# Adding D*x with GpSimd from a spread row of D instead of with TensorE's diagonal product, in a fused MoE / selective-scan / MoE kernel

## The chip, the cores and the metric

The kernel runs on one core of a Trainium2 chip. The metric is the device time of one execution in microseconds (us); the median of several executions is given. The engines are called PE (TensorE), DVE (VectorE), ACT (ScalarE), POOL (GpSimd) and SP (SyncE, which issues most of the DMAs). Each of them works through its own list of instructions in order, and they meet only at semaphores.

## The reference, cut to what matters

x has 4 batches of 512 tokens with 256 channels. A mixture-of-experts layer, a selective scan and a second mixture-of-experts layer follow one another, each on normalised rows and each added to x:

```python
x = x + 0.5 * ffn(layernorm(x))
x = x + scan(layernorm(x))          # 16 states for each channel
x = x + 0.5 * ffn(layernorm(x))

def scan(x):                        # x is already normalised here
    ...
    h = dA_t * h + dBx_t            # for each time step
    y_t = sum_n h[:, :, n] * C_t[n]
    return y + x * D                # D: one number for each of 256 channels
```

The change concerns the last line alone, x * D.

## The kernel before, in words

Tokens lie in 16 tiles of 128 rows (`x_sb`, and the normalised rows in `xn_no`, called `xn` in the code); four tiles make a batch. The first layer ends at about 110 us of the profiled execution, the scan layer runs from there to about 330 us, and the second layer fills the rest.

The scan layer's main part treats 64 states, s = 16 b + n, for batch b = 0 to 3 and n = 0 to 15. All of it is laid out by hand in loops `scan(b)`, one for each engine, and the place of an `if` in such a loop is the place of the work in the engine's order. For one state:

- ACT makes the decay `da` (128 partitions x 1024, for the 256 channels as two halves `k` of 512 time steps) three states ahead, and most of the inputs `dbx_t`.
- PE turns or multiplies the inputs into PSUM, `turn_dbx(s + 2)`, two states ahead. This is L1033 (transposes) or, for 22 of the states, L1040 (a product with a diagonal).
- DVE runs the recurrence over time, L1426, `hs[s]` from `da` and PSUM. `hs` is a ring of four, so it may not be more than four states ahead of POOL.
- POOL multiplies by C, L526: `gs[s % 2] = hs[s] * c_sb`, with two buffers of `gs`. It waits for DVE's `hs[s]` (`sc_h`) and for PE's use of `gs[s - 2]` (`sc_tp`).
- PE turns `gs[s]` back to rows and accumulates it over the 16 states of a batch in the two PSUM banks `YA`: `add(s)`, L1057, which waits for POOL's `gs[s]` (`sc_g`). In PE's order it stands as ..., `turn_dbx(s + 2)`, `add(s - 1)`, `turn_dbx(s + 3)`, `add(s)`, ...

After the 16th `add` of a batch, DVE adds `YA` to the rows in `x_sb`: `add_y(b)`, L1462, which stands behind the second scan of the next batch (its n = 1). Beside this, DVE, ACT and PE prepare the next batch (projections, dt, normalisation). POOL's other work in the loop is one addition of rows (L515, in batch 0) and small steps of layer norm (L455, L456, L463, L464) behind n = 5 of batch 0 and n = 3 of the others.

x * D is made by PE in `skip(b, i)`, L1066, at n = 5 to 8 of each batch: for tile i, both halves k of the turned rows `xnT` are multiplied with D's diagonal `d_diag` (in `q_sb`) and accumulated into `YA` between the `add`s. POOL makes the diagonals once, L545, after the first layer. The data of an fp32 product pass PE twice here, so two `matmul` calls show up as four records.

Of the kernel before, what the change touches and what calls it, by code (L numbers as in the profile page):

```python
# [15 lines left out]
ALU = mybir.AluOpType  # L16
ACT = mybir.ActivationFunctionType
# [6 lines left out]
P = 128  # L24
# [3 lines left out]
def macaron_kernel(nc, x, w_xT, w_dtT, b_dt, a_log, d_skip, router_w, gate_w, up_w, down_w,  # L28
                   sh_gate_w, sh_up_w, sh_down_w, out):
    BATCH, L, D = x.shape  # L30
# [3 lines left out]
    KC = D // P  # L34
    LT = L // P
    GT = BATCH * LT
# [6 lines left out]
    NR = WHOLE + MIXED  # L43
# [23 lines left out]
    rows = [nc.dram_tensor(f"rows{r}", [TOK, WIDE[r]], F32, kind="Internal").ap() for r in range(RUNS)]  # L67
# [9 lines left out]
    with ExitStack() as ctx:  # L77
        def sb(name, shape, dt=F32):
            return ctx.enter_context(nc.sbuf_tensor(name, shape, dt))

        def sem(name):
            return ctx.enter_context(nc.semaphore(name))


        x_sb = sb("x_sb", [P, GT, D])
        xn_no = sb("xn_no", [P, GT, D + 2])
        xnT = sb("xnT", [P, KC, TOK])
# [6 lines left out]
        d_sb = sb("d_sb", [P, KC])  # L94
# [4 lines left out]
        dtx_t = sb("dtx_t", [P, 2, LT, D])  # L99

        ident = sb("ident", [P, P])
# [45 lines left out]
        q_sb = sb("q_sb", [P, 2, F])  # L147
        h_sb = sb("h_sb", [P, 2, F])
        y_sb = sb("y_sb", [P, 4, D])
# [6 lines left out]
        xn = xn_no[:, :, 0:D]  # L156
# [13 lines left out]
        log_w = tt[:].rearrange("p u a t -> p u (a t)")  # L170
        lg_sb = log_w[:, 0]
        proj = th[0:R + 2 * N].rearrange("p u f -> p (u f)")
        d_diag = q_sb[:, 0].rearrange("p (k t) -> p k t", k=KC)
        b_t = h_sb[:, 0].rearrange("p (b i n) -> p b i n", b=BATCH, i=LT)
        sg_h = y_sb[:].rearrange("p a d -> p (a d)").rearrange("p (k t) -> p k t", k=KC)
        last = dbx_t[:, 1].rearrange("p i d -> p (i d)").rearrange("p (k t) -> p k t", k=KC)
# [8 lines left out]
        YA = bank[6:8]  # L185
# [18 lines left out]
        consts = sem("consts")  # L204
        pool_chain = sem("pool_chain")
        dve_chain = sem("dve_chain")
        ln_stats, ln_rstd, ln_xn, ln_tp, ln_xnT = (sem(f"ln_{s}") for s in ("stats", "rstd", "xn", "tp", "xnT"))
# [4 lines left out]
        sh_gu, sh_tanh, sh_mul, sh_hidden, sh_y, sh_x = (  # L212
            sem(f"sh_{s}") for s in ("gu", "tanh", "mul", "hidden", "y", "x"))
# [23 lines left out]
        sc_da, sc_act, sc_dve, sc_dbx, sc_h, sc_g, sc_tp, sc_x = (  # L237
            sem(f"sc_{s}") for s in ("da", "act", "dve", "dbx", "h", "g", "tp", "x"))
        sc_last = sem("sc_last")

        def pj_bank(b, k):

# [179 lines left out]
        def _(pool):  # L422
# [44 lines left out]
            def normalise(c, b, tiles=range(LT)):  # L467
                pool.wait_ge(ln_rstd, BATCH * c + b + 1)
                if (c, b) == (1, 1):
                    pool.wait_ge(ln_xn, GT + LT)  # L470
                for i in (LT * b + t for t in tiles):
                    nc.gpsimd.tensor_scalar(xn[:, i], x_sb[:, i, :], mv[:, i, 0:1], rstd[:, i:i + 1],
                                            ALU.subtract, ALU.mult).then_inc(ln_xn, 1)
# [37 lines left out]
            def combine(b):  # L511
                pool.wait_ge(sh_x, LT // 2 * (b + 1))
                pool.wait_ge(back_in[b], 16)
                tiles = slice(LT * b, LT * (b + 1))
                nc.gpsimd.tensor_tensor(x_sb[:, tiles], xn[:, tiles], x_sb[:, tiles], ALU.add).then_inc(back_x, 1)  # L515

            def scan(b):
                for n in range(N):
                    s = N * b + n
                    if last_one(s):  # L520
                        continue
                    pool.wait_ge(sc_h, s + 1)
                    pool.wait_ge(c_in[s % RING], 16 * (s // RING + 1))
                    if s >= 2:
                        pool.wait_ge(sc_tp, s - 1)
                    nc.gpsimd.tensor_tensor(gs[:, s % 2], hs[:, s % RING], c_sb[:, s % RING].unsqueeze(1).to_broadcast([P, KC, L]),  # L526
                                            ALU.mult).then_inc(sc_g, 1)
                    if b == 0 and n == 3:
                        combine(BATCH - 1)
                    if b == 0 and n == 5:  # L530
                        rstd_of(1, BATCH - 1)
                        shift(1, BATCH - 1)
                    if b > 0 and n == 3:
                        rstd_of(2, b - 1)
                    if b > 0 and n == 3:
                        shift(2, b - 1)
# [5 lines left out]
            pool.wait_ge(small_in, 16 * 4)  # L542
            pool.wait_ge(consts, 1)
            for k in range(KC):
                nc.gpsimd.tensor_scalar(d_diag[:, k, :], ident[:], d_sb[:, k:k + 1], None, ALU.mult).then_inc(consts, 1)  # L545
            for b in range(BATCH - 1):
                rstd_of(1, b)
            for b in range(1, BATCH - 1):
                normalise(1, b)
            for b in range(BATCH):  # L550
                scan(b)
            rstd_of(2, BATCH - 1)
# [4 lines left out]
        def _(act):  # L557
# [6 lines left out]
            def ln_copies(c, b):  # L564
                for q in range(2 * b, 2 * b + 2):
                    ln_copy(c, q)
# [183 lines left out]
                shared_gate(0, 2, fo)  # L750
            shared_gate(0, 3, 0)
            nc.scalar.preload_act_table_set(EXP_LN)
            ln_copies(1, 0)
            project_copy(0)
            for k in range(KC):
# [28 lines left out]
        def _(pe):  # L784
# [29 lines left out]
            def ln_batch(c, b):  # L814
                for q in range(2 * b, 2 * b + 2):
                    ln_transposes(c, q)
# [86 lines left out]
            def routed(r):  # L903
# [72 lines left out]
                down(NR - 2)  # L976
                down(NR - 1)

            def project(b):
                lo = b * L  # L980
                pe.wait_ge(ln_xnT, GT // 2 + 2 * b + 2)
                if b > 0:
                    pe.wait_ge(ln_xnT, (GT // 2 + 6, GT // 2 + 6, GT + 2)[b - 1])
                    pe.wait_ge(pj_dtx, 2 * b)
                for k in range(KC):
                    mm = nc.tensor.matmul(pj_bank(b, 0)[0:R + 2 * N, :], w_x[:, k, :], xnT[:, k, lo:lo + L], start=(k == 0), stop=(k == KC - 1))
                mm.then_inc(pj_all, 1)
# [70 lines left out]
                                              start=(s % N == 0 and i == 0), stop=(s % N == N - 1), is_transpose=True, skip_group_check=True)  # L1058
                mm.then_inc(sc_tp, 1)

            def skip(b, i):
                lo = b * L
                if b == 0:
                    pe.wait_ge(consts, 1 + KC)
                for k in range(KC):
                    nc.tensor.matmul(YA[k][:, i * P:(i + 1) * P], xnT[:, k, lo + i * P:lo + (i + 1) * P], d_diag[:, k, :],  # L1066
                                     start=False, stop=False, skip_group_check=True)

            def scan(b):
                more = b + 1 < BATCH  # L1070
                for n in range(N):
                    s = N * b + n
                    if more and n == 3:
                        project_bt(b + 1)
                    if b > 0 and n == 0:
                        add(s - 1)
                    if s + 2 < STATES:
                        turn_dbx(s + 2)
                    if s == 0:
                        shared_down(0, 3, (1,))  # L1080
                        ln_transposes(1, 5)
                    if last_one(s):
                        shared_gate_up(1, 1, 0, (0,))
                    if s == 1:
                        project(1)
                    if n > 0:
                        add(s - 1)
                    if not more and n in PIECES:
                        shared_piece(PIECES.index(n))
                    late = (2, 1, 0, 0)[b]  # L1090
                    if more and n in (late, late + 1):
                        project_z(b + 1, n - late)
                    if 5 <= n < 5 + LT:
                        skip(b, n - 5)
                    if more and n - int(b == 0) in (8, 10):
                        turn_dt(b + 1, (n - 8) // 2)
                    turn = 12 if more else 9
                    if b > 0 and n in (turn, turn + 1):
                        ln_transposes(2, 2 * (b - 1) + n - turn)
                    if (b, n) in ((0, 14), (1, N - 1)):  # L1100
                        project(b + 2)
                    if s in (N - 1, N):
                        ln_transposes(1, s - N + 7)
# [23 lines left out]
            shared_gate_up(0, 3, 0)  # L1127
            shared_down(0, 2, (0,))
            pe.wait_ge(small_in, 16 * 4)
            ln_batch(1, 0)  # L1130
            shared_down(0, 2, (1,))
            project(0)
# [38 lines left out]
        def _(dve):  # L1171
# [219 lines left out]
            def project_dtx(b, h):  # L1391

                dve.wait_ge(pj_tp, 2 * b + h + 1)
                src = (YA[h] if b == 0 else T).rearrange("p (i d) -> p i d", i=2)
                nc.vector.tensor_tensor(dtx_t[:, b % 2, 2 * h:2 * h + 2, :], src, xn[:, LT * b + 2 * h:LT * b + 2 * h + 2, :],  # L1395
                                        ALU.mult).then_inc(pj_dtx, 1)
# [60 lines left out]

            def add_y(b):
                dve.wait_ge(sc_tp, N * (b + 1))
                for k in range(KC):  # L1460
                    rows = x_sb[:, b * LT:(b + 1) * LT, k * P:(k + 1) * P]
                    nc.vector.tensor_tensor(rows, rows, YA[k].rearrange("p (i d) -> p i d", i=LT), ALU.add).then_inc(sc_x, 1)  # L1462
# [93 lines left out]
```

## Time and profile before

| | |
|---|---|
| median of 3 runs | 435.62 us (433.93 to 435.76) |
| the profiled execution, its own time | 438.39 us |
| span of the profiled execution, first to last instruction | 436.7 us |
| mean granted clock of TensorE | 0.986 of full speed |
| busy: PE, DVE, ACT, POOL | 403.5 us (92%), 327.0 (75%), 276.6 (63%), 267.4 (61%) |

The busy shares are means over stages of different kinds; for the change only the scan stage counts, from about 144 us to 326 us, where all four engines are close to full. Times of instructions below are counted from the start of the span.

### The profile page before, as it was taken

What the parts mean: (1) busy time and instruction counts of PE and PEld (TensorE: products, weight loads), DVE (VectorE), ACT (ScalarE), POOL (GpSimd) and SP (SyncE); (2) the same over time, 40 slices, a digit from 0 to 9 for tenths busy, and PEclk for the clock granted to TensorE, in tenths of its full rate; (3) what the DMA queues carried; (4) which work ended last, traced back from release to release, by engine and by line L of the source; (5) the groups of instructions that cost most, each with busy time, mean ns of one, the idle gap of its engine ahead of it and who ended that gap; (6) DMA issues with size and microseconds to landing.
All of it is one profiled execution on the core that took longest, in us unless ns stands there. A gap on an engine that the chain in (4) does not pass through costs nothing. (4 is left out here: it accounts for less than half of the span.)

```text
span 436.7 us, 8333 instructions
## 1 busy us (share of the span) xinstructions
PE 403.5 (92%) x2716; PEld 280.8 (64%) x2716; DVE 327.0 (75%) x510; ACT 276.6 (63%) x516; POOL 267.4 (61%) x210
## 2 busy tenths in 40 slices
PE   5899899999977998999899999999999899899995
PEld 5436444444444978988898799888974556344452
DVE  4678555554287979999999999999897775456552
ACT  1431365655138789999999999998952210656552
POOL 6203446643329569888979798979881006577543
PEclk9899999999999799999999999999999999999999
DMA  8949214943424133864454448533310534344411
GB/s 251 386 153 284 59 44 136 306 155 134 152 68 97 53 96 119 145 124 151 134 111 109 144 133 144 134 117 119 124 50 0 192 99 116 93 120 136 120 52 49
DMA packets 50809, 56.85 MB, mean 130 GB/s; under 512 B 16327, under 2 KB 35596, under 8 KB 50768
## 3 DMA queue, kind: packets, MB, share of 16 engines
q1 hardware_dynamic: 46624, 45.78, 36.3%
q0 software_dynamic: 4144, 10.54, 8.1%
q8 instruction: 23, 0.38, 0.4%
q14 instruction: 18, 0.15, 0.1%
HBM read 41.14 MB, written 16.48 MB: 132 GB/s over the span
## 5 line engine op out<-in xcount | busy, mean ns | idle before, releaser
L526 POOL TENSOR_TENSOR gs<-hs,c_sb 128x1024 f32<-128x1024 f32 x63 | 148.2, 2373 | 26.2 <-PE bank L1057 17.4
L1426 DVE TENSOR_TENSOR_SCAN hs<-da,bank 128x1024 f32<-128x1024 f32 x64 | 143.9, 2273 | 3.7 <-PE bank L1033 1.9
L663 ACT ACTIVATE da<-dt_sb,a_neg 128x511 f32<-128x511 f32 x128 | 84.2, 709 | 1.6 <-DVE dt_sb L1389 1.2
L1057 PE MATMUL bank<-ident,gs 128*128 128x128 f32 x504 | 65.5, 273 | 2.0 <-POOL gs L526 2.0
L679 ACT ACTIVATE dbx_t<-dtx_t,h_sb 128x256 f32<-128x256 f32 x153 | 65.1, 495 | 0.8 <-DVE dtx_t L1395 0.7
L1057 PEld LDWEIGHTS bank<-ident,gs 128*128 128x128 f32 x504 | 56.7, 141 | 5.0 <-POOL gs L526 3.8
L882 PE MATMUL bank<-xnT,w_gu 128*128 128x512 f32 x112 | 51.6, 609 | 0.0
L1033 PE MATMUL bank<-ident,dbx_t 128*128 128x128 f32 x336 | 46.0, 282 | 5.1 <-DVE dbx_t L1410 1.8
L480 POOL DMA_INDIRECT da<-rows,row_token x29 | 30.1, 1038 | 30.4 <-issue 30.1
L1033 PEld LDWEIGHTS bank<-ident,dbx_t 128*128 128x128 f32 x336 | 39.0, 145 | 8.7 <-issue 5.3
L591 ACT ACTIVATE th<-bank,da 128x256 f32<-128x256 f32 x36 | 17.1, 474 | 43.0 <-PE bank L921 30.4
L921 PE MATMUL bank<-w_gu,tt 128*128 x72 | 35.6, 616 | 3.1 <-ACT tt L596 2.2
L480 POOL DMA_INDIRECT da<-rows,row_half x14 | 15.3, 1094 | 35.6 <-DVE row_token L1302 27.2
L501 POOL DMA_INDIRECT token_out<-y_sb,row_token x18 | 19.0, 1056 | 29.4 <-DVE y_sb L1343 26.6
L1333 DVE TENSOR_TENSOR h_sb<-th,bank 128x256 f32<-128x256 f32 x36 | 15.1, 420 | 27.9 <-ACT th L591 27.7
L918 PE MATMUL bank<-w_gu,tt 128*32 x72 | 34.3, 598 | 1.4 <-ACT tt L596 1.4
L882 PEld LDWEIGHTS bank<-xnT,w_gu 128*128 128x128 f32 x112 | 20.9, 193 | 22.5 <-issue 22.3
L918 PE MATMUL bank<-dtx_t,tt 128*32 128x512 f32 x72 | 34.3, 598 | 0.0
L574 ACT ACTIVATE hs<-bank 128x512 f32<-128x512 f32 x10 | 6.0, 597 | 40.0 <-PE bank L882 34.6
L596 ACT ACTIVATE tt<-bank 128x512 f32<-128x512 f32 (+1 forms) x40 | 22.1, 553 | 13.8 <-PE bank L936 12.5
L501 POOL DMA_INDIRECT out<-y_sb,row_token x18 | 18.7, 1040 | 16.8 <-DVE y_sb L1346 9.4
L562 ACT ACTIVATE xnT<-bank 128x512 f32<-128x512 f32 x24 | 13.9, 589 | 20.2 <-PE bank L810 20.1
(184 smaller groups left out, 772.3 us busy)
## 6 DMA issues: line engine op xcount, KB each, us to landing
c_sb<-c_dram SPq DMA_DIRECT2D x64, 256.0 KB, 3.5
rows<-xn_no SPq DMA_DIRECT2D x8, 516.0 KB, 5.3
diag_dram<-dbx_t SPq DMA_DIRECT2D x6, 512.0 KB
routing<-diag_dram SPq DMA_DIRECT2D x11, 256.0 KB, 3.5
slot_m<-diag_dram SPq DMA_DIRECT2D x11, 256.0 KB, 3.5
rows<-xn_no SPq DMA_DIRECT2D x1, 2064.0 KB, 9.1
x_sb<-in_x SPq DMA_DIRECT2D x4, 512.0 KB, 6.7
w_gu<-in_gate_w SPq DMA_DIRECT2D x2, 1024.0 KB, 10.0
```

The lines of the kernel that those rows point to most:

```text
L480: nc.gpsimd.indirect_dma_start(out=xr[:, u, lo:hi], out_offset=None, in_=source, in_offset=bass.IndirectOffsetOnAxis(ap=row, axis=0), boun ...
L501: nc.gpsimd.indirect_dma_start(out=rows_back, out_offset=bass.IndirectOffsetOnAxis(ap=row_token[:, TILE[j]:TILE[j] + 1], axis=0), in_=y_sb ...
L526: nc.gpsimd.tensor_tensor(gs[:, s % 2], hs[:, s % RING], c_sb[:, s % RING].unsqueeze(1).to_broadcast([P, KC, L]), ALU.mult).then_inc(sc_g, 1)
L596: nc.scalar.activation(tt[:, (j + 1) % 2, lo:hi], T[:, lo * P:hi * P].rearrange("p (a t) -> p a t", t=P), ACT.Copy).then_inc(ff_tpc, 1)
L663: nc.scalar.activation(da[:, s % RING, k, 1:L], dt_sb[:, k, seq(s // N)][:, 1:L], ACT.Exp, scale=a_neg[:, k, s % N:s % N + 1]).then_inc(sc ...
L679: step = nc.scalar.activation(plain_buffer(s)[:, i, :], dtx_t[:, b % 2, i, :], ACT.Copy, scale=b_t[:, b, i, n:n + 1])
L882: last = nc.tensor.matmul(shared_banks(r, b, fo)[h], w_gu[:, k, SHARED, h * F + fo * P:h * F + (fo + 1) * P], xnT[:, k, b * L:(b + 1) * L] ...
L918: last = nc.tensor.matmul(H[j % 2][part, :], tt[:, j % 2, 2 + k, part], gu_part(i, g)[:, k, :] if g else w, start=(k == 0), stop=(k == KC ...
L921: last = nc.tensor.matmul(H[j % 2][:, :], tt[:, j % 2, 2 + k], w, start=(k == 0), stop=(k == KC - 1))
L1033: mm = nc.tensor.transpose(DBX[s % 2][:, k, i * P:(i + 1) * P], plain_buffer(s)[:, i, k * P:(k + 1) * P], ident[:])
L1057: mm = nc.tensor.matmul(YA[k][:, i * P:(i + 1) * P], products[:, k, i * P:(i + 1) * P], ident[:], start=(s % N == 0 and i == 0), stop=(s % ...
L1426: nc.vector.tensor_tensor_scan(hs[:, s % RING].rearrange(flat), da[:, s % RING].rearrange(flat), DBX[s % 2][:, :, :].rearrange(flat), 0.0, ...
```

## The change

Of the diff, the lines that only name tiles and semaphores are cut, and the rest is whole:

```diff
-        d_diag = q_sb[:, 0].rearrange("p (k t) -> p k t", k=KC)
+        d_rep = q_sb[:, 0].rearrange("p (k t) -> p k t", k=KC)
+        d_row = q_sb[:, 1]
...
+            def spare(b):
+                return (dtx_t[:, 1] if b == 0 else y_sb[:])
+
+            def skip_product(b, lo, hi):
+                if b == 0:
+                    pool.wait_ge(d_ready, 1)
+                    pool.wait_ge(ln_xn, GT + LT)
+                elif b == 1:
+                    pool.wait_ge(sh_y, GT // 2)
+                else:
+                    pool.wait_ge(sk_add, 2 * (b - 1))
+                    pool.wait_ge(ln_xn, 2 * GT)
+                row = d_row.unsqueeze(1).to_broadcast([P, hi - lo, D])
+                nc.gpsimd.tensor_tensor(spare(b)[:, lo:hi], xn[:, LT * b + lo:LT * b + hi], row, ALU.mult).then_inc(sk_mul, hi - lo)
+
+            def skip_add(b, lo, hi):
+                pool.wait_ge(sk_mul, LT * b + hi)
+                rows = x_sb[:, LT * b + lo:LT * b + hi]
+                nc.gpsimd.tensor_tensor(rows, rows, spare(b)[:, lo:hi], ALU.add).then_inc(sk_add, (hi - lo) // 2)
...
                     if b == 0 and n == 3:
                         combine(BATCH - 1)
+                    if b < BATCH - 1 and n in (6, 8):
+                        skip_product(b + 1, n - 6, n - 4)
+                    if b < BATCH - 1 and n in (10, 12):
+                        skip_add(b + 1, n - 10, n - 8)
...
             for k in range(KC):
-                nc.gpsimd.tensor_scalar(d_diag[:, k, :], ident[:], d_sb[:, k:k + 1], None, ALU.mult).then_inc(consts, 1)
+                nc.gpsimd.tensor_scalar(d_rep[:, k, :], ident[:], 0.0, d_sb[:, k:k + 1], ALU.mult, ALU.add).then_inc(consts, 1)
...
                 normalise(1, b)
+            skip_product(0, 0, LT)
+            skip_add(0, 0, LT)
             for b in range(BATCH):
                 scan(b)
...
             nc.scalar.preload_act_table_set(EXP_LN)
+            act.wait_ge(d_turned, 1)
+            nc.scalar.activation(d_row, YA[1][:, 0:D], ACT.Copy).then_inc(d_ready, 1)
             ln_copies(1, 0)
...
+            def turn_d():
+                pe.wait_ge(consts, 1 + KC)
+                pe.wait_ge(ff_yc, NR)
+                for k in range(KC):
+                    mm = nc.tensor.transpose(YA[1][:, k * P:(k + 1) * P], d_rep[:, k, :], ident[:])
+                mm.then_inc(d_turned, 1)
...
-            def skip(b, i):
-                lo = b * L
-                if b == 0:
-                    pe.wait_ge(consts, 1 + KC)
-                for k in range(KC):
-                    nc.tensor.matmul(YA[k][:, i * P:(i + 1) * P], xnT[:, k, lo + i * P:lo + (i + 1) * P], d_diag[:, k, :],
-                                     start=False, stop=False, skip_group_check=True)
...
-                    if 5 <= n < 5 + LT:
-                        skip(b, n - 5)
...
             pe.wait_ge(small_in, 16 * 4)
+            turn_d()
             ln_batch(1, 0)
...
             def project_dtx(b, h):
                 dve.wait_ge(pj_tp, 2 * b + h + 1)
+                if b == 1:
+                    dve.wait_ge(sk_add, 2)
...
             def add_y(b):
                 dve.wait_ge(sc_tp, N * (b + 1))
+                dve.wait_ge(sk_add, 2 * (b + 1))
```

A row of D on all partitions is made once: POOL spreads each half of D along the columns (`d_rep`), PE turns it into PSUM (`turn_d`), ACT copies it to `d_row`. POOL multiplies the normalised rows of a batch by that row into a spare buffer and adds the product to `x_sb`. For batch 0 this is done whole before the scan; for batches 1 to 3 in halves of two tiles (128 x 512) during the scan of the batch before, the two products behind n = 6 and n = 8, the two additions behind n = 10 and n = 12. In the scan of batch 3 POOL gets nothing new.

The order of POOL's instructions around the scan of batch 0 shows this. Before, from the layer-norm rows (`normalise`, here L472) through the 16 products with C (`gs`, L526) of batch 0 into batch 1:

```order
67 L472 TENSOR_SCALAR xn_no<-x_sb,mv,rstd 128x256 x8
68 L526 TENSOR_TENSOR gs<-hs,c_sb 128x1024 x4
69 L515 TENSOR_TENSOR x_sb<-xn_no,x_sb 128x1024
70 L526 TENSOR_TENSOR gs<-hs,c_sb 128x1024 x2
71 L455 TENSOR_SCALAR var_eps<-mv 128x4
72 L456 TENSOR_TENSOR rstd<-var_eps,neg_half 128x4
73 L463 TENSOR_TENSOR mean_rstd<-mv,rstd 128x4
74 L464 TENSOR_SCALAR mean_rstd<-mean_rstd 128x4
75 L526 TENSOR_TENSOR gs<-hs,c_sb 128x1024 x14
```

And in the changed kernel, whose products with C have line L549, products with D line L533 and additions line L538:

```order
67 L474 TENSOR_SCALAR xn_no<-x_sb,mv,rstd 128x256 x8
68 L533 TENSOR_TENSOR dtx_t<-xn_no,q_sb 128x1024
69 L538 TENSOR_TENSOR x_sb<-x_sb,dtx_t 128x1024
70 L549 TENSOR_TENSOR gs<-hs,c_sb 128x1024 x4
...
77 L549 TENSOR_TENSOR gs<-hs,c_sb 128x1024
78 L533 TENSOR_TENSOR y_sb<-xn_no,q_sb 128x512
79 L549 TENSOR_TENSOR gs<-hs,c_sb 128x1024 x2
80 L533 TENSOR_TENSOR y_sb<-xn_no,q_sb 128x512
81 L549 TENSOR_TENSOR gs<-hs,c_sb 128x1024 x2
82 L538 TENSOR_TENSOR x_sb<-x_sb,y_sb 128x512
83 L549 TENSOR_TENSOR gs<-hs,c_sb 128x1024 x2
84 L538 TENSOR_TENSOR x_sb<-x_sb,y_sb 128x512
85 L549 TENSOR_TENSOR gs<-hs,c_sb 128x1024 x7
```

Two whole instructions now stand ahead of POOL's first product with C, and four half ones stand between the products of n = 6 and n = 13.

On PE, at n = 5 to 8 of batch 0, the diagonal products (L1066) stood directly behind the `add`s (L1057), before:

```order
364 L1057 MATMUL bank<-ident,gs 128x128 x8
365 L1066 MATMUL bank<-q_sb,xnT 128x128 x2
366 L1033 MATMUL bank<-ident,dbx_t 128x128 x8
367 L1057 MATMUL bank<-ident,gs 128x128 x8
368 L1066 MATMUL bank<-q_sb,xnT 128x128 x2
369 L1040 MATMUL bank<-routing,dtx_t 128x128 x8
```

In the changed kernel (`add` is L1095, the turning of the inputs L1071 and L1078) they are gone:

```order
365 L1095 MATMUL bank<-ident,gs 128x128 x8
366 L1071 MATMUL bank<-ident,dbx_t 128x128 x8
367 L1095 MATMUL bank<-ident,gs 128x128 x8
368 L1078 MATMUL bank<-routing,dtx_t 128x128 x8
```

And ahead of the scan PE has two transposes of D (L1014) between the shared expert's product (L893) and the turning of the normalised rows (L841):

```order
333 L893 MATMUL bank<-w_dn,gs 128x256 x4
334 L1014 MATMUL bank<-ident,q_sb 128x128 x2
335 L841 MATMUL bank<-ident,xn_no 128x128 x8
336 L893 MATMUL bank<-w_dn,gs 128x256 x4
337 L1024 MATMUL bank<-xnT,w_x 96x512 x2
```

There, only line 334 is new; the others stood in the same order.

## Rows read from the trace of the kernel before

**Rows 1.** Busy time in four stretches of the scan, one for each batch.
```profile
core 0: us, PE busy (x) PEld busy (x) DVE busy (x) ACT busy (x) POOL busy (x), PEclk, DMA share, GB/s
164.90:195.46 30.56, 28.59 (x244) 26.79 (x242) 30.14 (x24) 29.88 (x59) 28.16 (x16) 1.00 0.64 130
195.46:238.07 42.61, 40.54 (x342) 37.41 (x340) 41.57 (x38) 41.62 (x81) 36.78 (x20) 1.00 0.48 130
238.07:281.40 43.33, 42.64 (x348) 38.51 (x348) 43.23 (x38) 42.53 (x85) 38.48 (x21) 1.00 0.54 133
281.40:326.30 44.90, 42.52 (x339) 39.91 (x340) 41.58 (x35) 39.28 (x80) 39.35 (x21) 1.00 0.34 111
```

**Rows 2.** Groups by line, 140 to 325 us: shapes, count | busy us, mean ns | idle before.
```profile
L526 POOL TENSOR_TENSOR gs<-hs,c_sb 128x1024 f32<-128x1024 f32 x63 | 148.2, 2373 | 26.2 <-PE bank L1057 17.4 <-DVE hs L1426 8.5
...
L1066 PE MATMUL bank<-q_sb,xnT 128*128 128x128 f32 x64 | 9.8, 275 | 0.0
...
L515 POOL TENSOR_TENSOR x_sb<-xn_no,x_sb 128x1024 f32<-128x1024 f32 x1 | 2.2, 2168 | 0.0
...
L463 POOL TENSOR_TENSOR mean_rstd<-mv,rstd 128x4 f32<-128x4 f32 x4 | 0.8, 203 | 0.3
```

**Rows 3.** Timeline of POOL in the scan: start us, us, instructions [idle before].
```profile
188.22 7.29 POOL L526 TENSOR_TENSOR gs<-hs,c_sb 128x1024 f32<-128x1024 f32 x3 [0.24 <-PE bank L1057]
...
231.31 14.01 POOL L526 TENSOR_TENSOR gs<-hs,c_sb 128x1024 f32<-128x1024 f32 x6 [0.24 <-PE bank L1057]
...
267.28 2.37 POOL L526 TENSOR_TENSOR gs<-hs,c_sb 128x1024 f32<-128x1024 f32 x1 [0.60 <-DVE hs L1426]
270.35 4.71 POOL L526 TENSOR_TENSOR gs<-hs,c_sb 128x1024 f32<-128x1024 f32 x2 [0.71 <-PE bank L1057]
275.30 14.02 POOL L526 TENSOR_TENSOR gs<-hs,c_sb 128x1024 f32<-128x1024 f32 x6 [0.24 <-PE bank L1057]
```

**Rows 4.** Timeline of PE in the scan, places where products with C are used.
```profile
191.53 1.04 PE L1057 MATMUL bank<-ident,gs 128*128 128x128 f32 x8
192.41 1.88 PE L986 MATMUL bank<-xnT,w_x 128*96 128x512 f32 x4
194.12 1.04 PE L1033 MATMUL bank<-ident,dbx_t 128*128 128x128 f32 x8
...
241.70 1.04 PE L1057 MATMUL bank<-ident,gs 128*128 128x128 f32 x8
...
284.72 1.09 PE L1057 MATMUL bank<-ident,gs 128*128 128x128 f32 x8 [1.22 <-POOL gs L526]
```

**Rows 5.** Timeline of DVE at the same places and in batch 3.
```profile
195.46 2.28 DVE L1426 TENSOR_TENSOR_SCAN hs<-da,bank 128x1024 f32<-128x1024 f32 x1
...
242.78 1.28 DVE L1462 TENSOR_TENSOR x_sb<-x_sb,bank 128x512 f32<-128x512 f32 x2
...
285.85 1.29 DVE L1462 TENSOR_TENSOR x_sb<-x_sb,bank 128x512 f32<-128x512 f32 x2
...
308.13 6.67 DVE L1426 TENSOR_TENSOR_SCAN hs<-da,bank 128x1024 f32<-128x1024 f32 x3 [0.82 <-PE bank L1040]
315.61 6.92 DVE L1426 TENSOR_TENSOR_SCAN hs<-da,bank 128x1024 f32<-128x1024 f32 x3 [0.81 <-PE bank L1040]
```

**Rows 6.** Busy time around POOL's products of n = 6 to 12, columns as in the first group.
```profile
169.80:188.22 18.42, 18.36 (x166) 18.04 (x165) 18.00 (x15) 17.74 (x35) 16.53 (x9) 1.00 0.66 117
216.47:226.35 9.88, 9.09 (x80) 8.85 (x80) 9.85 (x9) 9.54 (x20) 7.12 (x3) 1.00 0.59 136
```

**Rows 7.** Timeline of PE ahead of the scan and at its first `add`.
```profile
123.89 1.16 PE L810 MATMUL bank<-ident,xn_no 128*128 128x128 f32 x8
...
126.61 1.88 PE L986 MATMUL bank<-xnT,w_x 128*96 128x512 f32 x4
...
155.14 1.04 PE L1057 MATMUL bank<-ident,gs 128*128 128x128 f32 x8
```

**Rows 8.** Timeline of POOL at its first products with C.
```profile
146.78 4.88 POOL L526 TENSOR_TENSOR gs<-hs,c_sb 128x1024 f32<-128x1024 f32 x2 [4.11 <-DVE hs L1426]
```

**Rows 9.** The addition of L515 as DVE makes it, groups by line, 118 to 128 us.
```profile
L1362 DVE TENSOR_TENSOR x_sb<-xn_no,x_sb 128x1024 f32<-128x1024 f32 x2 | 2.4, 1223 | 3.4 <-DMA xn_no<-token_out 3.4
```

## What the change will do: the prediction

> **What bounds the kernel now.** I read the page first, whose busy shares (PE 92%) make a removal on PE look like a gain, and then the busy time by stretch, because the change lives in the scan alone. There [rows 1] the reader is to see that no engine has room: in the stretches of batches 0 to 2 DVE is busy 30.14 of 30.56 us, 41.57 of 42.61 and 43.23 of 43.33, so together it is idle for only 0.42 + 1.04 + 0.10 = 1.56 us. Whatever PE saves there, the recurrence on DVE can come forward by no more than that. In batch 3 DVE is idle for 44.90 - 41.58 = 3.3 us. POOL is idle for 2.40, 5.83 and 4.85 us in batches 0 to 2, together 13.1 us. Third I read the groups by line and the timelines of POOL, PE and DVE, to find which wait ends last at the end of each batch.
>
> **What is removed.** The 64 records of D's product cover 9.8 us of PE [rows 2], 2.45 us for each batch. In batches 0 to 2 I give this nothing: the work that hides it is DVE's, which is full [rows 1]; if that cover were gone, up to 1.56 us would come back. In batch 3 two scans start late and name a PE product as the releaser, with 0.82 and 0.81 us of idle time [rows 5]. Both stand behind D's products in PE's order (n = 5 to 8, then the turning two states ahead), so what PE saves by then, 1.2 us for two of the four tiles and 2.45 for all, covers both. Gain in batch 3: 0.82 + 0.81 = 1.6 us. The end of the scan and the second layer follow from there and move with it.
>
> **What is added ahead of the scan.** PE's two transposes of D stand where PE goes from one block to the next without idle time up to the projection [rows 7]. Eight transposes take 1.16 us there, so two take 0.3 us, and the projection, from which the decays of the first states follow, comes 0.3 us later. Cost: 0.3 us. ACT's copy waits for these transposes, but ACT's next work is the copy of the next transposed rows, which is released by PE about as much later; I give it nothing, at most 0.4 us. POOL's spreading of D takes the place of an instruction of the same size. The full product and addition of batch 0 are priced by the nearest rows, 2.37 us for the product with C (it too repeats an operand) and 2.17 us for an addition of rows [rows 2], together 4.5 us. POOL was idle for 4.11 us ahead of its first product with C [rows 8], so that product comes about 0.5 us late, ends at about 149.7, and is not used by PE before 155.14 [rows 7]. Cost: nothing; without that cover 0.5 us.
>
> **The price of one half instruction on POOL.** No row shows 128 x 512. From below it is half of the whole addition, 1.08 us. From above it is the fixed part of a tiny instruction, 0.20 us for 4 columns, and the slope to the product: 0.20 + (2.37 - 0.20) x 508/1020 = 1.28 us; for the addition the same sum gives 1.18 [rows 2]. I take 1.2 us, hence 4.8 us for the four of a batch and 14.4 us for twelve.
>
> The Trainium skill (GPSIMD Engine Reference, "Engine selection") speaks against the change: elementwise products and sums of two tiles belong on VectorE, as GpSimd takes about twice as long. The trace agrees: the same addition of 1024 columns takes 1.22 us on DVE and 2.17 us on POOL [rows 2, 9]. Its figure in "Elementwise — side-by-side cycle accounting", 4497 ns for 2048 columns, would make a half instruction an estimated 1.12 us, 0.3 us less for each batch, and the forecast about 1 us lower.
>
> **Where this goes.** POOL's four new instructions stand between the products of n = 6 and n = 13. Queued behind them on POOL are the products with C; PE's `add(s)` waits for these, and behind that `add` in PE's order stands the turning of the input for a scan on DVE, and at the end of a batch `add_y`. So I follow how late POOL is, in each batch, once its idle time between these products is used up.
>
> *Batch 2* is the clearest. POOL's idle time behind the first new product is 0.60 + 0.71 + 0.24 = 1.55 us, and then six products run without a gap from 275.30 [rows 3]. With 4.8 us of new work, the second and later of these six are 4.8 - 1.55 = 3.25 us late. The fourth of the six ends now at 275.30 + 4 x 14.02/6 = 284.65, and the `add` that needs it starts at 284.72, after 1.22 us in which PE waited for just that; `add_y` follows at 285.85, directly behind the `add` [rows 4, 5]. There is no slack here: `add_y`, and the scan behind it, come 3.2 us later.
>
> *Batch 0.* In the stretch from the product of n = 6 to that of n = 13 POOL is idle for 18.42 - 16.53 = 1.9 us [rows 6]. The product of n = 13 starts 4.8 - 1.9 = 2.9 us later, at 191.1 instead of 188.22 [rows 3], and ends at 193.5. PE's `add` of it began at 191.53, so PE stands still for 2.0 us with a projection and the turning at 194.12 behind it; that turning then ends at about 197.1, and the scan that started at 195.46 waits for it [rows 4, 5]. Cost 1.6 to 1.75 us (the `add_y` behind it needs one more late product); I take 1.7.
>
> *Batch 1.* Behind n = 6, POOL is idle for 9.88 - 7.12 = 2.76 us before the products of n = 10 [rows 6], which holds the two products with D, 2.4 us. The two additions then meet 0.24 us of idle time and six products without a gap [rows 3]: 2.15 us late. The fourth of these six (n = 15) ends at 231.31 + 4 x 14.01/6 = 240.65 now and at 242.8 then; its `add` started at 241.70, and `add_y` right behind it at 242.78 [rows 4, 5]. Cost 242.8 - 241.7 = 1.1 us at least; I take 1.2.
>
> **Sum:** 0.3 + 1.7 + 1.2 + 3.2 - 1.6 = +4.8 us. Each loss is kept, as DVE has nothing to catch up with [rows 1]. Against the profiled execution's own 438.39 us that is 443.2 us. That execution was 2.8 us above the median of the runs shown, so against the median: 435.62 + 4.8 = **440.4 us**, slower by 1.1%. The new waits on DVE (`add_y` and the projection of batch 1 for the additions on POOL) cost nothing, as the additions of batch 0 end where POOL's first product starts, at about 147 us, far ahead of both, and the others end a batch ahead; of SP's loads of C, which wait for POOL's products, each has three other products between its release and its use.
>
> **The rivals.**
>
> *The slack takes it up.* Summed up, 14.4 us of new work meet 13.1 us of idle time in the three batches. If POOL could use all of it, being late in one place without holding up PE, the loss in the scan would be 14.4 - 13.1 = 1.3 us, and the sum 0.3 + 1.3 - 1.6 = 0.0: 435.6 us, no change that can be measured (about 0.5% can be told for this kernel, 2.2 us). For it: a `hs` ring of four, and DVE itself only waits for POOL when it is four states ahead. Against it: two buffers of `gs` and an in-order PE tie POOL to within two states, and in batch 2 PE waits for POOL already [rows 4]. At 1.08 us for a half instruction the losses of the three batches are each 0.4 to 0.5 us smaller, 439.1 us, still slower. Chance 0.18.
>
> *PE was the bound after all,* which ends on the other side. If PE's time sets the recurrence through its queue of `add`s and turnings, each batch gives back what DVE idles: 1.56 + 3.3 = 4.9 us, less 0.3 us ahead of the scan, and 431.0 us. For it: PE is busy 42.64 of 43.33 us in batch 2 [rows 1]. It decides only if POOL's half instruction fits into what POOL idles behind n = 6 without any lag, in batch 2 at 1.55/4 = 0.4 us or less; the nearest rows say three times that. Chance 0.08.
>
> *It costs more.* If PE and POOL don't meet as smoothly as I assume, and half of the idle time that I let POOL use in the three batches (1.9 + 2.65 + 1.55 = 6.1 us) isn't there, the loss grows by 3 us, to 443.4 us; if each half instruction takes 1.4 us, it grows by 12 x 0.2 = 2.4 us. If both, it is 446 us. Chance 0.10 for more than 443.5 us.
>
> **How the numbers follow.** The forecast, POOL late at the end of each batch, has 0.64, with a range of its own from 437.8 to 443.5 us. Slower by over 0.5% (above 437.8 us) are it and the dearer case, 0.73 with a little taken off for its lower edge; faster by over 0.5% (below 433.4) is the second rival, 0.08; the rest, 0.19, lies between. The range from 435.4 to 444.5 us leaves out the second rival, about half of the first and a part of the third.
>
> **What would show each step right or wrong.** In the changed profile the half instructions should take 1.1 to 1.3 us; POOL should be busy for nearly all of batches 0 to 2, with PE's `add` at n = 13 to 15 waiting for POOL, and DVE idle ahead of the scans around each `add_y` by 1 to 3 us, most in batch 2. In batch 3 the two waits of 0.8 us for PE should be gone. The scan should start 0.3 us later. I am wrong if DVE's idle time in batches 0 to 2 stays below 2 us, which would mean that POOL's lateness is soaked up, or if the half instructions take under 0.8 us.

## The result, and the profile after

The changed kernel takes 441.44 us (median of 4 runs, 440.28 to 446.01) against 435.4 us before: a ratio of 1.016 with a 95% interval of 1.012 to 1.020. By the two medians alone the difference is 6.0 us, 1.4%; of the four runs the one of 446.01 us stands apart. The forecast was 440.4 us, slower. The profiled execution of the changed kernel took 441.93 us (span 440.2). Its busy times, from the page:

```profile
PE 395.7 (90%) x2654; PEld 270.1 (61%) x2654; DVE 327.3 (74%) x510; ACT 277.2 (63%) x517; POOL 285.6 (65%) x224
```

PE is 7.8 us less busy and POOL 18.2 us more. Groups by line, 140 to 330 us (shapes, count | busy us, mean ns | idle before):

```profile
L549 POOL TENSOR_TENSOR gs<-hs,c_sb 128x1024 f32<-128x1024 f32 x63 | 148.0, 2367 | 12.4 <-PE bank L1095 10.1 <-DVE hs L1457 2.0
L1457 DVE TENSOR_TENSOR_SCAN hs<-da,bank 128x1024 f32<-128x1024 f32 x64 | 144.2, 2274 | 5.0 <-PE bank L1071 4.0 <-PE bank L1078 0.8
...
L1095 PE MATMUL bank<-ident,gs 128*128 128x128 f32 x496 | 65.3, 275 | 10.2 <-POOL gs L549 10.0
```

The wait has turned round. POOL's idle time ahead of its products fell from 26.2 us [rows 2] to 12.4, and PE's `add` (L1095) now waits 10.0 us for POOL, where it waited 2.0 before:

```profile
L1057 PE MATMUL bank<-ident,gs 128*128 128x128 f32 x504 | 65.5, 273 | 2.0 <-POOL gs L526 2.0
```

The new instructions, by line (count: ns min/median/max, first and last start):

```profile
L533 POOL TENSOR_TENSOR y_sb<-xn_no,q_sb x6: 1169/1178/1182, 168.8 to 267.8; 128x512 f32<-128x512 f32 x6
...
L538 POOL TENSOR_TENSOR x_sb<-x_sb,y_sb x6: 1267/1272/1287, 180.4 to 279.5; 128x512 f32<-128x512 f32 x6
```

A product takes 1.18 us and an addition 1.27, 4.9 us for a batch where 4.8 were taken.

To see where the time went I measure each batch of the scan on DVE, from one event to the next: the layer-norm statistics in batch 0, and the four `add_y`. The timeline of DVE, before (its other two `add_y` are in [rows 5]):

```profile
163.20 1.41 DVE L1182 BATCH_NORM_STATS2 stats<-x_sb 128x6 f32<-128x256 f32 x4 [0.53 <-POOL x_sb L515]
...
197.66 1.26 DVE L1462 TENSOR_TENSOR x_sb<-x_sb,bank 128x512 f32<-128x512 f32 x2
...
329.14 1.28 DVE L1462 TENSOR_TENSOR x_sb<-x_sb,bank 128x512 f32<-128x512 f32 x2 [0.91 <-PE bank L1057]
```

And after:

```profile
159.87 1.41 DVE L1211 BATCH_NORM_STATS2 stats<-x_sb 128x6 f32<-128x256 f32 x4 [0.53 <-POOL x_sb L517]
...
193.67 2.29 DVE L1457 TENSOR_TENSOR_SCAN hs<-da,bank 128x1024 f32<-128x1024 f32 x1 [1.46 <-PE bank L1071]
195.88 1.26 DVE L1494 TENSOR_TENSOR x_sb<-x_sb,bank 128x512 f32<-128x512 f32 x2
...
242.77 1.28 DVE L1494 TENSOR_TENSOR x_sb<-x_sb,bank 128x512 f32<-128x512 f32 x2 [1.48 <-PE bank L1095]
...
285.10 2.29 DVE L1457 TENSOR_TENSOR_SCAN hs<-da,bank 128x1024 f32<-128x1024 f32 x1 [0.83 <-PE bank L1071]
288.87 1.28 DVE L1494 TENSOR_TENSOR x_sb<-x_sb,bank 128x512 f32<-128x512 f32 x2 [1.48 <-PE bank L1095]
...
332.16 1.28 DVE L1494 TENSOR_TENSOR x_sb<-x_sb,bank 128x512 f32<-128x512 f32 x2 [0.91 <-PE bank L1095]
```

The differences of these starts, in us, with those of the experiments below (one profiled execution of each kernel; the last column is from all its runs):

| kernel | batch 0 | batch 1 | batch 2 | batch 3 | sum | median, ratio to before |
|---|---|---|---|---|---|---|
| before | 34.46 | 45.12 | 43.07 | 43.29 | 165.94 | 435.4 |
| changed | 36.01 | 46.89 | 46.10 | 43.29 | 172.29 | 441.44, 1.016 |
| no work on POOL in the scan | 34.45 | 45.10 | 43.07 | 43.27 | 165.89 | 434.94, 1.001 (0.999 to 1.003) |
| POOL's work and PE's both | 36.03 | 46.89 | 46.17 | 43.28 | 172.37 | 440.91, 1.014 (1.011 to 1.017) |
| POOL's work moved | 34.45 | 45.11 | 43.87 | 43.30 | 166.73 | 436.31, 1.003 (1.000 to 1.006) |
| changed, n = 11 of batch 3 to PE | 35.98 | 48.05 | 46.12 | 41.71 | 171.86 | 440.87, 1.011 (1.006 to 1.015) |
| before, n = 11 of batch 3 to PE | 34.45 | 45.11 | 43.08 | 43.47 | 166.11 | 434.88, 1.000 (0.998 to 1.002) |
| moved, n = 11 of batch 3 to PE | 34.45 | 45.42 | 43.87 | 41.74 | 165.48 | 434.03, 0.999 (0.996 to 1.001) |
| the same, one addition earlier | 34.45 | 45.44 | 43.78 | 41.72 | 165.39 | 433.58, 0.999 (0.997 to 1.001) |

The loss is +1.55, +1.77 and +3.03 us in batches 0 to 2 and nothing in batch 3, 6.35 us in all. The profiled execution of before started its scan stage later for a reason outside the change (last section), so its span is only 3.5 us shorter.

How it comes about is seen at the ends of the batches. POOL's timeline after:

```profile
186.30 1.27 POOL L538 TENSOR_TENSOR x_sb<-x_sb,y_sb 128x512 f32<-128x512 f32 x1
187.54 14.24 POOL L549 TENSOR_TENSOR gs<-hs,c_sb 128x1024 f32<-128x1024 f32 x6
...
273.57 1.27 POOL L538 TENSOR_TENSOR x_sb<-x_sb,y_sb 128x512 f32<-128x512 f32 x1
274.81 4.68 POOL L549 TENSOR_TENSOR gs<-hs,c_sb 128x1024 f32<-128x1024 f32 x2
279.46 1.27 POOL L538 TENSOR_TENSOR x_sb<-x_sb,y_sb 128x512 f32<-128x512 f32 x1
280.69 11.63 POOL L549 TENSOR_TENSOR gs<-hs,c_sb 128x1024 f32<-128x1024 f32 x5
```

In batch 1, at POOL's products of n = 8 and n = 10, which still wait for PE, and at those of n = 13 to 15 and the next two:

```profile
218.56 2.37 POOL L549 TENSOR_TENSOR gs<-hs,c_sb 128x1024 f32<-128x1024 f32 x1 [0.43 <-PE bank L1095]
...
224.84 2.37 POOL L549 TENSOR_TENSOR gs<-hs,c_sb 128x1024 f32<-128x1024 f32 x1 [0.44 <-PE bank L1095]
...
234.31 11.64 POOL L549 TENSOR_TENSOR gs<-hs,c_sb 128x1024 f32<-128x1024 f32 x5
```

And PE's:

```profile
189.95 1.09 PE L1095 MATMUL bank<-ident,gs 128*128 128x128 f32 x8 [1.59 <-POOL gs L549]
190.88 1.88 PE L1024 MATMUL bank<-xnT,w_x 128*96 128x512 f32 x4
192.60 1.04 PE L1071 MATMUL bank<-ident,dbx_t 128*128 128x128 f32 x8
...
239.05 1.09 PE L1095 MATMUL bank<-ident,gs 128*128 128x128 f32 x8 [0.37 <-POOL gs L549]
239.98 1.88 PE L1024 MATMUL bank<-xnT,w_x 128*96 128x512 f32 x4
241.70 1.04 PE L1095 MATMUL bank<-ident,gs 128*128 128x128 f32 x8
...
287.74 1.09 PE L1095 MATMUL bank<-ident,gs 128*128 128x128 f32 x8 [1.22 <-POOL gs L549]
```

In batch 0, POOL's product of n = 13 starts at 187.54 and ends at about 189.9; PE has waited 1.59 us for it; a projection (L1024) and the turning of an input (L1071, 192.60) stand behind it, and the scan of DVE that needs the latter starts at 193.67 after 1.46 us of idle time. That is the chain of the prediction, row by row. At the end of batch 2 the last `add`s wait for POOL (1.22 us at 287.74) and `add_y` for the `add`.

### The profile page after: what moved, and what is told of

Same layout as the page of the kernel before. It is cut to its first block and busy times, and to the rows that moved or that the text cites. A ratio compares the mean times of both kernels' runs of the same rounds, so it can differ in the third digit from the quotient of the medians.

```text
span 440.2 us, 8239 instructions
## 1 busy us (share of the span) xinstructions
PE 395.7 (90%) x2654; PEld 270.1 (61%) x2654; DVE 327.3 (74%) x510; ACT 277.2 (63%) x517; POOL 285.6 (65%) x224
## 5 line engine op out<-in xcount | busy, mean ns | idle before, releaser
L549 POOL TENSOR_TENSOR gs<-hs,c_sb 128x1024 f32<-128x1024 f32 x63 | 148.0, 2367 | 12.4 <-PE bank L1095 10.1
L1095 PE MATMUL bank<-ident,gs 128*128 128x128 f32 x504 | 66.3, 275 | 10.2 <-POOL gs L549 10.0
L1095 PEld LDWEIGHTS bank<-ident,gs 128*128 128x128 f32 x504 | 55.9, 141 | 16.5 <-POOL gs L549 15.6
L708 ACT ACTIVATE dbx_t<-dtx_t,h_sb 128x256 f32<-128x256 f32 x153 | 65.2, 496 | 0.8 <-DVE dtx_t L1426 0.7
L1071 PE MATMUL bank<-ident,dbx_t 128*128 128x128 f32 x336 | 44.1, 274 | 5.4 <-issue 3.0
L1071 PEld LDWEIGHTS bank<-ident,dbx_t 128*128 128x128 f32 x336 | 37.5, 141 | 8.8 <-issue 7.5
L893 PE MATMUL bank<-w_dn,gs 128*128 128x256 f32 x96 | 22.2, 382 | 2.2 <-DVE gs L1230 1.0
```

The lines of the kernel that those rows point to most:

```text
L708: step = nc.scalar.activation(plain_buffer(s)[:, i, :], dtx_t[:, b % 2, i, :], ACT.Copy, scale=b_t[:, b, i, n:n + 1])
L893: last = nc.tensor.matmul(shared_out(r, q)[:, i * D:(i + 1) * D], hidden_rows(r, b)[:, k, t * P:(t + 1) * P], w_dn[:, k, SHARED, :], start ...
L1071: mm = nc.tensor.transpose(DBX[s % 2][:, k, i * P:(i + 1) * P], plain_buffer(s)[:, i, k * P:(k + 1) * P], ident[:])
L1095: mm = nc.tensor.matmul(YA[k][:, i * P:(i + 1) * P], products[:, k, i * P:(i + 1) * P], ident[:], start=(s % N == 0 and i == 0), stop=(s % ...
```

## The experiments

Two theories were tested. Mine, after the result: the loss is POOL's lateness at the ends of batches 0 to 2, PE's saved time is hidden behind DVE there, and in batch 3 something other than PE (I supposed ACT) ends last. The rivals: POOL's work costs by its sum, whatever its place; or PE's saving is worth something and pays part of a larger loss. Each kernel was timed in 5 rounds, and the four of the first group and the three of the second each shared the runs of before (434.98 and 434.75 us).

**No work on POOL in the scan.** The twelve half instructions are dropped, and with them D*x for the rows of batches 1 to 3.

```diff
-                    if b < BATCH - 1 and n in (6, 8):
-                        skip_product(b + 1, n - 6, n - 4)
-                    if b < BATCH - 1 and n in (10, 12):
-                        skip_add(b + 1, n - 10, n - 8)
...
-                dve.wait_ge(sk_add, 2 * (b + 1))
+                if b == 0:
+                    dve.wait_ge(sk_add, 2)
```

> The changed kernel without POOL's twelve half instructions in the scan: D*x is left out of the rows of batches 1 to 3 (batch 0 keeps it). It shows what taking D's products off PE is worth alone. If POOL's lateness is the whole loss and PE's saving is hidden, batches 0 to 2 keep the lengths of the kernel before, within 0.3 us each, and the time is that of before, 435 to 436 us. If my gain of 1.6 us in batch 3 were there, 433.5 to 434.5 us. If PE set the pace (the second rival), all of DVE's idle time comes back, 4.9 us, about 431 us. In the changed kernel batch 3 was as long as before, 42.1 us from its third scan to its last addition; I expect that again, with ACT's work as what ends last there.

Measured 434.94 us, a ratio of 1.001. Each batch is as long as before, within 0.02 us. Taking 2.45 us of PE's work out of each batch is worth nothing in any of them, batch 3 too; the gain of 1.6 us that I had forecast there doesn't exist, and the second rival falls.

**Both.** PE's products are put back beside POOL's work.

```diff
+            def skip(b, i):
+                lo = b * L
+                for k in range(KC):
+                    nc.tensor.matmul(YA[k][:, i * P:(i + 1) * P], xnT[:, k, lo + i * P:lo + (i + 1) * P], d_rep[:, k, :],
+                                     start=False, stop=False, skip_group_check=True)
...
+                    if 5 <= n < 5 + LT:
+                        skip(b, n - 5)
```

> The changed kernel with PE's products of D put back at n = 5 to 8, beside POOL's work (PE multiplies by the spread rows of D instead of the diagonal, and both are added, so the rows hold more than D*x). If PE's 2.45 us a batch are hidden, the time is that of the changed kernel within 0.5 us, about 441.4 us. If PE's saving had paid back part of a larger loss on POOL, this is 2 to 5 us slower, 443.5 to 446 us.

Measured 440.91 us; the batches are those of the changed kernel within 0.07 us. So PE's saving pays back none of POOL's loss, and the loss is POOL's alone.

**Moved.** The same twelve instructions at other places.

```diff
-                    if b < BATCH - 1 and n in (6, 8):
-                        skip_product(b + 1, n - 6, n - 4)
-                    if b < BATCH - 1 and n in (10, 12):
-                        skip_add(b + 1, n - 10, n - 8)
+                    if b < BATCH - 1:
+                        for at, lo in (((1, 0), (1, 2)), ((1, 0), (2, 2)), ((1, 0), (2, 2)))[b]:
+                            if n == at:
+                                skip_product(b + 1, lo, lo + 2)
+                        for at, lo in (((8, 0), (10, 2)), ((6, 0), (8, 2)), ((8, 0), (9, 2)))[b]:
+                            if n == at:
+                                skip_add(b + 1, lo, lo + 2)
```

> The changed kernel with the same twelve half instructions at other places, where POOL idles in the trace of before: the products behind n = 1 and 2 (batch 0: both behind n = 1), the additions behind n = 8 and 10 (batch 0), 6 and 8 (batch 1), 8 and 9 (batch 2). If what costs is POOL's lateness at the end of a batch, the losses of the three batches fall from 1.6, 1.8 and 3.0 us to about 0.3, 0.5 and 1.0, and the time to about 437 us (436.3 to 438). If what costs is the sum of POOL's work, which is the same here, it stays at 440.5 to 442 us.

Measured 436.31 us. The loss of batches 0 and 1 is gone and that of batch 2 is 0.80 us, 0.8 us in all in place of 6.35, with the same work on POOL. So nearly all of the 6.35 us was the price of the places and not of the sum of the work; what is left in batch 2 is taken up in the last experiment. By the medians the kernel is 1.3 us above before. The busy time by stretch between the same events (columns PE, PEld, DVE, ACT, POOL):

```profile
core 0: us, PE busy (x) PEld busy (x) DVE busy (x) ACT busy (x) POOL busy (x), PEclk, DMA share, GB/s
...
196.14:241.25 45.11, 41.51 (x336) 36.90 (x334) 44.08 (x40) 44.13 (x87) 44.48 (x25) 1.00 0.52 130
241.25:285.12 43.87, 40.24 (x330) 36.05 (x329) 42.93 (x37) 43.07 (x84) 42.88 (x25) 1.00 0.50 131
```

In batch 1 POOL is now busy 44.48 of 45.11 us without having become the bound.

**n = 11 of batch 3 from ACT to PE, on the changed kernel.** First what made me suppose ACT. In the changed kernel the idle time of DVE in batch 3 is still there, 0.21 + 0.81 + 0.56 = 1.58 us ahead of three scans where it was 0.82 + 0.81 us ahead of two; the timelines of PE, ACT and DVE there:

```profile
311.80 1.04 PE L1095 MATMUL bank<-ident,gs 128*128 128x128 f32 x8
313.83 1.06 PE L1071 MATMUL bank<-ident,dbx_t 128*128 128x128 f32 x8 [0.99 <-issue]
...
316.04 1.95 PE L1078 MATMUL bank<-slot_m,dtx_t 128*128 128x128 f32 x16
```
```profile
306.72 0.38 ACT L613 ACTIVATE th<-bank 128x256 f32<-128x256 f32 x1 [1.87 <-PE bank L929]
...
308.72 1.69 ACT L708 ACTIVATE dbx_t<-dtx_t,h_sb 128x256 f32<-128x256 f32 x4
...
312.04 1.69 ACT L708 ACTIVATE dbx_t<-dtx_t,h_sb 128x256 f32<-128x256 f32 x4
```
```profile
314.93 2.29 DVE L1457 TENSOR_TENSOR_SCAN hs<-da,bank 128x1024 f32<-128x1024 f32 x1 [0.21 <-PE bank L1071]
318.03 2.29 DVE L1457 TENSOR_TENSOR_SCAN hs<-da,bank 128x1024 f32<-128x1024 f32 x1 [0.81 <-PE bank L1078]
320.88 4.67 DVE L1457 TENSOR_TENSOR_SCAN hs<-da,bank 128x1024 f32<-128x1024 f32 x2 [0.56 <-PE bank L1071]
```

PE stands still for 0.99 us before the turning at 313.83, that of n = 11. The profile's "issue" names nobody, but the instruction that makes these inputs, ACT's L708, ends at 313.73. From 306.72 on ACT works without a gap, and its inputs for one state come 3.3 us behind those of the last (308.72, 312.04). The turning is then followed by the product that releases DVE late. So I gave one state's inputs to PE:

```diff
-    DIAG = ((6, 7, 9, 10, 12, 14),) + ((4, 6, 7, 9, 11, 13),) * 2 + ((3, 6, 9, 12),)
+    DIAG = ((6, 7, 9, 10, 12, 14),) + ((4, 6, 7, 9, 11, 13),) * 2 + ((3, 6, 9, 11, 12),)
```

> The changed kernel with one more state of batch 3 (n = 11) taken from ACT, which makes its inputs in four instructions of 0.42 us, and given to PE's product with a diagonal, 0.9 us more for PE. If ACT is what took the gain of batch 3, the stretch from the third scan of batch 3 to its last addition falls from 42.1 to 40.4 to 41.3 us and the time by about 1.2 us to 440.2 us. If PE or POOL sets that stretch, it stays or grows by up to 0.9 us.

Measured 440.87 us. Batch 3 took 41.71 us, 1.58 us less, though PE got work. (Batch 1 of this profiled execution is 1.2 us longer than in the changed kernel, for the clock, last section; the median, over six runs from 437.63 to 442.89 us, fell by 0.6 us only, where 1.2 were expected.) So in the changed kernel ACT's work was what held batch 3.

**The same edit on the kernel before.** As a control, the last diff alone, on the kernel with D's products on PE.

> The kernel before, D's products on PE, with the state n = 11 of batch 3 given from ACT to PE's product with a diagonal. If taking D's products off PE is what makes room for it, PE now holds 2.45 + 0.9 us more than in the run with the same edit on the changed kernel, and batch 3 (from the layer-norm statistics in it to its last addition, 43.3 us from one batch's addition to the next) stays at 42.8 to 44 us, the time at 435 to 436 us. If ACT alone bounds batch 3 and PE has room for both, batch 3 falls to 41.7 us here too, and the time to about 433.5 us; then the change gains nothing even there.

Measured 434.88 us, batch 3 43.47 us, 0.18 us longer. So take work from PE alone and nothing comes (first run); give ACT's work to a PE that still has D's products, and nothing comes (this run); do both and 1.58 us come. This run also loads PE with 0.9 us more, so it doesn't show what relieving ACT without that would give. The rows point the same way: the busy time, columns as in the moved run, in the kernel before, for 15 us from where ACT starts after its last longer wait, and then in the changed kernel from the same point (306.72):

```profile
303.71:318.71 15.00, 14.99 (x136) 14.67 (x134) 12.90 (x8) 15.00 (x32) 13.23 (x6) 1.00 0.38 123
...
306.72:322.00 15.28, 13.52 (x120) 12.87 (x118) 13.20 (x8) 15.28 (x33) 13.64 (x7) 1.00 0.44 121
```

Before, PE and ACT both have no idle time there; in the changed kernel PE has, and ACT still has none.

**Moved, with n = 11 of batch 3 to PE.** The two diffs together.

> The changed kernel with POOL's half instructions at the places of the moved run and the state n = 11 of batch 3 given from ACT to PE. If the two effects are independent, the scan is 0.8 us longer than before by POOL's lateness in batch 2 and 1.6 us shorter in batch 3: 434.3 us against 435.0 before, a ratio of 0.998. If POOL's work, which in batch 3 is the same, binds once ACT is relieved, 435 to 436 us.

Measured 434.03 us, a ratio of 0.999 (0.996 to 1.001). The scan is 0.46 us shorter than before (165.48 against 165.94), where 0.8 were expected. Batches 2 and 3 came as expected; batch 1 is 0.3 us longer than in the moved run, and in it the granted clock of TensorE fell (the last columns: clock, DMA share, GB/s):

```profile
205.00:215.00 10.00, 8.15 (x65) 7.48 (x64) 9.04 (x8) 9.97 (x20) 9.84 (x8) 0.94 0.49 144
215.00:225.00 10.00, 9.54 (x77) 9.30 (x77) 9.97 (x8) 9.67 (x20) 8.70 (x5) 0.89 0.38 95
```

In the moved run's batch 1 it stayed at 1.00, as shown above. In the run that follows it fell at the same place (0.92 and 0.91 in the same stretches), and batch 1 is as long as here, 45.44 us.

**One addition of batch 2 earlier.**

```diff
-                        for at, lo in (((8, 0), (10, 2)), ((6, 0), (8, 2)), ((8, 0), (9, 2)))[b]:
+                        for at, lo in (((8, 0), (10, 2)), ((6, 0), (8, 2)), ((2, 0), (9, 2)))[b]:
```

> As the run before it in this list, with one of the two additions of batch 2 moved from behind n = 8 to behind n = 2, where POOL idles more. If lateness at the end of the batch is the loss, batch 2 loses its 0.8 us lag (1.3 us less work behind n = 8) but pays where POOL has 0.7 us more than it idles by n = 3: 0.2 to 0.7 us of loss, 433.7 to 434.2 us. If the place doesn't matter, as the run before it.

Measured 433.58 us, a ratio of 0.999 (0.997 to 1.001). Batch 2 gained 0.09 us only; its loss of 0.71 us stands at the upper end of what I expected. Early in the batch PE now waits 1.40 us for POOL, where it waited 0.25 in the run before, and POOL is busy for 43.45 of the batch's 43.78 us. In this batch the sum binds too: POOL's idle time in it was 4.85 us before [rows 1], and the new work is 4.9 us, so no idle time is over that another place could use. This version has the lowest median of those tried, and it can't be told from the kernel before.

## Why the prediction was right, point by point

- *POOL late at the end of a batch* was right, and shown from both sides: without POOL's work the loss is gone, with PE's work put back it stays, at other places it falls from 6.35 to 0.8 us. By batch: 1.7 forecast and 1.55 measured, 1.2 and 1.77, 3.2 and 3.03. In batch 1 I took 1.2 from POOL's product of n = 15 alone. It ends at 234.31 + 3 x 11.64/5 = 241.29, which, counted from the `add_y` before it, is 2.4 us late where 2.15 was forecast: POOL left 0.43 + 0.44 = 0.87 us of idle time unused at n = 8 and 10, and my sum only 0.36. By that the `add` would come about 1.4 us late. It comes 1.78 late, for what I left out: the `add` of n = 14, at 239.05, waits for POOL too, and the projection of 1.7 us between the two in PE's order moves with it.
- *Nothing for PE in batches 0 to 2, as DVE is full,* was right: 0.02 us at most.
- *The gain of 1.6 us in batch 3* was wrong, and the step that failed is its reading of [rows 5]: two waits that name PE as the releaser. That said who came last, not who would come next. ACT, 3.3 us of work for a state there without a gap, was ready to take PE's place and did; DVE's idle time stayed at 1.58 us. The forecast was 4.8 us of loss, and 6.45 came, 6.35 in the scan and 0.1 ahead of it; without this term it would have been 6.4. That this is so near is in part luck: batch 1 lost 0.57 us more than its term, and batch 0, batch 2 and the stretch ahead of the scan together 0.52 us less.
- *The half instruction at 1.2 us* was 1.18 and 1.27. *The transposes of D:* PE's next block starts 0.22 us after theirs, where 0.3 was taken, and from DVE's first normalised rows to its first scan it is 21.56 us after (121.66 to 143.22) and 21.46 before, so 0.1 us of it reached the scan. *The full product and addition of batch 0* cost nothing, as forecast: the first product with C starts 2.8 us behind the first scan (146.00, 143.22) and was 2.4 us behind it (146.78, 144.41), and the way from the first scan to the statistics of batch 0 is 16.65 us in the changed kernel and as long in the kernel before with n = 11 of batch 3 to PE (142.95 to 159.60), where the clock stayed at full too. POOL's rows after:

```profile
141.33 2.19 POOL L533 TENSOR_TENSOR dtx_t<-xn_no,q_sb 128x1024 f32<-128x1024 f32 x1
143.67 2.38 POOL L538 TENSOR_TENSOR x_sb<-x_sb,dtx_t 128x1024 f32<-128x1024 f32 x1
146.00 4.69 POOL L549 TENSOR_TENSOR gs<-hs,c_sb 128x1024 f32<-128x1024 f32 x2
```

- *The rivals.* That slack takes the work up is wrong at these places and nearly right at others (0.8 us for the moved run). That PE was the bound is wrong. That it costs more is wrong in the main: the half instructions cost about what I took, and POOL used its idle time as I let it in batches 0 and 2; in batch 1 it left 0.5 us more, where this rival had 3 us in all.

## What to carry to other kernels

Where several engines are full together, work moved from one to another is priced by its place on the receiving engine: look for the idle time in front of each of its instructions, follow the lateness through the buffers to the next in-order queue, and put the work where the gaps are, as far as their sum holds it. A busy share of 90% on the giving engine says nothing of a gain if another engine has no idle time in that stretch. And when a wait names its releaser, ask which engine would come next before counting the wait as a gain; here taking work from either engine alone gave nothing.

## What the runs showed of the hardware

In these runs TensorE's granted clock falls to its lower level, 1.2 GHz, in some executions and not in others: the 28 runs of the kernel before that the second group of experiments shares and that took 433 to 438 us have mean granted clocks from 0.982 to 1.000 of full speed. The two falls shown here stand behind a stretch in which PE did little. In the run that gave n = 11 to PE on the changed kernel this happened in batch 1; the stretches, and PE's timeline:

```profile
215.00:218.00 3.00, 1.05 (x6) 1.05 (x7) 3.00 (x3) 3.00 (x7) 3.00 (x3) 0.88 0.80 211
218.00:221.00 3.00, 3.00 (x17) 3.00 (x17) 2.97 (x4) 3.00 (x6) 1.61 (x1) 0.55 0.31 76
```
```profile
216.95 3.51 PE L1078 MATMUL bank<-slot_m,dtx_t 128*128 128x128 f32 x16 [1.96 <-DVE hs L1457]
```

PE had been idle for 1.96 us; the granted clock was 0.88 and then 0.55 of full speed, and the product that takes 1.95 us elsewhere took 3.51. POOL's product behind it waited 2.07 us for PE, where it waited 0.43 in the changed kernel, and batch 1 grew by 1.2 us. The idle time alone doesn't decide it: at the same place of the changed kernel, whose instructions are the same up to there, PE was idle as long, and the clock stayed at full:

```profile
215.46 2.05 PE L1078 MATMUL bank<-slot_m,dtx_t 128*128 128x128 f32 x16 [1.97 <-DVE hs L1457]
```

The same fall hit the profiled execution of before ahead of the scan, at 142 to 148 us:

```profile
139.00:142.00 3.00, 1.10 (x8) 0.86 (x8) 2.14 (x5) 2.63 (x6) 3.00 (x4) 0.89 0.00 0
142.00:145.00 3.00, 2.88 (x14) 2.91 (x15) 2.97 (x5) 2.15 (x6) 0.66 (x1) 0.50 0.00 0
145.00:148.00 3.00, 3.00 (x14) 2.91 (x13) 3.00 (x3) 3.00 (x6) 1.23 (x1) 0.50 0.00 0
```

There the way from the first scan to the statistics of batch 0 is 18.8 us (144.41 to 163.20), and 16.65 in the changed kernel's (143.22 to 159.87), where the clock stayed at full. What stands ahead differs too: DVE's first normalised rows start between 120.05 and 123.20 us in the nine profiled executions, and at 122.95 and 121.50 in the two whose code is the same up to there and holds D's products on PE. This is why the spans of two single executions don't give the price of this change, and the stretches of the scan do.

Two prices on GpSimd were not as expected: an addition into its own first operand takes longer (1.27 us for 512 columns, 2.38 for 1024) than a product with a row repeated over the tiles (1.18 and 2.19), though [rows 2] had an addition of 1024 columns at 2.17 and a product with a repeated operand at 2.37. No run here tells why.
